# Attention without a gate: transposed scores and their exponentials one slot later

## What is computed

```
scores = einsum('bhqd,bhkd->bhqk', q, k) * scale
attn   = softmax(scores, axis=-1)
out    = einsum('bhqk,bhkd->bhqd', attn, v)      # then  out @ wo (+ bo)
```

## Time and profile before

| | |
|---|---|
| median of the runs | 5419.02 us |
| the profiled execution's own time | 5403.87 us |
| its span, first to last instruction | 5402.1 us |
| granted TensorE clock over the span | 0.866 of full speed |
| busy share PE / VectorE / ScalarE / GpSimd | 75% / 79% / 51% / 60% |
| f0, a1 and x1 together | about 1560 us |

### The profile page before, as it was taken

One profiled execution on the slowest core, in us unless ns is written; L12 is line 12 of the kernel. 1 busy time (PEld: TensorE's weight loads), 2 busy tenths in 40 slices (PEclk: granted clock), 3 DMA queues, 4 the chain that ended last, 5 costly groups with the idle time before them and its releaser, 6 DMA issues. The chain is left out here.

```text
span 5402.1 us, 104475 instructions
## 1 busy us (share of the span) xinstructions
PE 4058.6 (75%) x29692; PEld 2332.1 (43%) x29692; DVE 4293.4 (79%) x8421; ACT 2777.7 (51%) x6469; POOL 3230.1 (60%) x3458
## 2 busy tenths in 40 slices
PE   5888778887888778874888678883555787788853
PEld 2333333333333333332666446663554665566632
DVE  5999999999999999995788867764255777666668
ACT  4555555555555555552777533444563445344435
POOL 5888888888888888874777633325453222233335
PEclk8998998889989999886999878995786888899975
DMA  2111111011111111111666366654125555376521
GB/s 84 67 46 57 69 69 69 38 67 69 69 57 45 69 69 69 42 61 34 111 106 105 62 111 106 109 90 151 55 88 98 94 95 93 70 120 111 104 56 31
DMA packets 320201, 420.84 MB, mean 78 GB/s; under 512 B 40000, under 2 KB 301713, under 8 KB 309137
## 3 DMA queue, kind: packets, MB, share of 16 engines
q1 hardware_dynamic: 315536, 408.35, 32.6%
q0 software_dynamic: 4352, 8.95, 0.5%
HBM read 307.65 MB, written 109.58 MB: 77 GB/s over the span
## 5 line engine op out<-in xcount | busy, mean ns | idle before, releaser
L2202 POOL TENSOR_TENSOR m_h<-m_dtu,m_Bb 128x512 f32<-128x512 f32 x1024 | 1595.2, 1586 | 150.8 <-PE bank L1835 148.2
L1835 PE MATMUL bank<-m_h,ident 128*128 128x512 f32 x2048 | 1254.2, 704 | 400.3 <-DVE m_h L2101 393.2
L1835 PEld LDWEIGHTS bank<-m_h,ident 128*128 128x128 f32 x2048 | 373.1, 212 | 1084.6 <-DVE m_h L2101 930.6
L2095 DVE TENSOR_TENSOR_SCAN m_h<-m_dA,m_h 128x512 f32<-128x512 f32 x512 | 771.3, 1506 | 0.5
L2101 DVE TENSOR_TENSOR m_h<-m_h,bank 128x512 f32<-128x512 f32 x1024 | 672.6, 657 | 13.1 <-PE bank L1828 13.1
L2095 DVE TENSOR_TENSOR_SCAN m_h<-bank,m_h 128x512 f32<-128x512 f32 x512 | 620.6, 1212 | 16.3 <-ACT bank L1983 9.5
L1983 ACT ACTIVATE m_dA<-m_dt,m_A 128x512 f32<-128x512 f32 x512 | 366.9, 717 | 354.5 <-DVE m_h L2095 347.7
L1983 ACT ACTIVATE bank<-m_dt,m_A 128x512 f32<-128x512 f32 x512 | 352.5, 688 | 379.2 <-DVE m_h L2095 273.3
L688 DVE TENSOR_REDUCE x_nm<-bank 128x4 f32<-128x308 f32 x512 | 242.7, 474 | 177.9 <-PE bank L359 175.0
L531 ACT ACTIVATE x_sm<-bank,x_nm 128x77 f32<-128x77 f32 x1024 | 317.7, 335 | 62.3 <-DVE x_nm L688 61.9
L688 DVE TENSOR_REDUCE f_nm<-bank 128x4 f32<-128x512 f32 x256 | 175.8, 688 | 123.8 <-PE bank L359 123.1
(11 more groups left out here) (425 smaller groups left out, 10404.8 us busy)
## 6 DMA issues: line engine op xcount, KB each, us to landing
m_Bb<-m_B SPq DMA_DIRECT2D x32, 4096.0 KB, 12.1
x_Ks<-x_k_parts SPq DMA_DIRECT2D x32, 462.0 KB
x_q_parts<-x_qp SPq DMA_DIRECT2D x32, 384.0 KB, 4.1
x_Qs<-x_q_parts SPq DMA_DIRECT2D x32, 384.0 KB
f_Ks<-f_k_parts SPq DMA_DIRECT2D x16, 768.0 KB
a_Ks<-a_k_parts SPq DMA_DIRECT2D x16, 768.0 KB
x_xp<-x_stage SPq DMA_DIRECT2D x32, 256.0 KB
x_Qs<-x_q_parts SPq DMA_DIRECT2D x32, 256.0 KB
```

Of the source, the lines that this page charges most:

```text
L1835: pe.matmul(banks[4 + c], ident[:], h[:, k % RING, :], start=(s == 0), stop=(s == NS - 1)).then_inc(s_ya.sem, 1)
L2095: v.tensor_tensor_scan(h[:, k % RING, :], decays[k % AHEAD], h[:, k % RING, :], 0.0, ALU.mult, ALU.add).then_inc(s_h.sem, 1)
L2202: pool.tensor_tensor(h[:, k % RING, :], dtu[:, d, c, :], Bb[:, d, s, :], ALU.mult).then_inc(s_dB.sem, 1)
```

## The change

The transposed scores and their exponentials of chunk c run two slots behind the slot of `turn_max` instead of one. The maxima's transpose, the plain scores, the values and everything else keep their place. A helper says which item and chunk belong to a slot; for the gated stage x0 nothing is changed.

```diff
+    T_AT = 2
...
+        def turned_chunk(c):
+            return (1, c - T_AT) if c >= T_AT else (2, c - T_AT + 4)
...
@@ tensor, step
-                elif c == 0:
-                    if live(2):
-                        shifted(b - 2, (lb - 2) % 8, 3)
-                    if live(1):
+                else:
+                    k, chunk = turned_chunk(c)
+                    if live(k):
+                        shifted(b - k, (lb - k) % 8, chunk)
+                    if c == 0 and live(1):
                         turn_max(b - 1, (lb - 1) % 8)
-                elif live(1):
-                    shifted(b - 1, (lb - 1) % 8, c - 1)
@@ scalar, step
-                    if c == 0 and live(2):
-                        exp(b - 2, (lb - 2) % 8, 3)
-                    if c > 0 and live(1):
-                        exp(b - 1, (lb - 1) % 8, c - 1)
+                    k, chunk = turned_chunk(c)
+                    if live(k):
+                        exp(b - k, (lb - k) % 8, chunk)
```

## The result

| | before | after |
|---|---|---|
| median of the runs | 5420.0 us (5417.2 to 5424.55, 4 runs) | 5328.65 us (5324.35 to 5332.97, 4 runs) |
| ratio | | 0.9836 (95%: 0.982 to 0.9852) |
| the profiled execution's own time, span | 5403.87, 5402.1 us | 5331.78, 5330.1 us |
| granted TensorE clock | 0.866 | 0.875 |

The changed kernel is 91 us faster; 45 were forecast (5374 us, range 5345 to 5400). Sign and place were right; the gain is twice what was forecast. The two profiled executions differ by 72 us, because the one of before was 16 us under its median and the one of after 3 us over.

What follows compares the result with a forecast made beforehand. PE was taken as mostly the bound, sometimes waiting for VectorE. Gains 21 (a1) + 18 (x1) + 1 (f0) - 1 (drain) + 5 (clock) = 44, rounded to 45 us, gave 5374 us, range 5345 to 5400.

Steps and rivals of the forecast that it cites:

- a1: 21: Stage a1: direct gain of 21 us from PE's vanished waits for `nmT`, 10 at loop turns, 10 inside turns, 1 at the end.
- the clock: 5: Mainly a1's loop turns: less idle time brings PE back to 2.4 GHz sooner; 5 us taken, bounds 0 and 7.
- f0: 1.1 us at most: Stage f0: PE's wait for `nmT` at L377 is 1.1 us in all, of which 1 us was taken as gain.
- x1: 18: Stage x1: all 19.6 us of PE's waits for `nmT` vanish, less 1.6 for the stack load: 18 us gained.
- ceiling of the direct gain: PE's waits for `nmT` at L377 in f0, a1 and x1, in all 58.2 us, 1.1% of the time.
- Place 2, last items of a group, 0 us: Last items of a1's groups, 11 waits, about 6.6 us: PE arrives earlier and waits longer for VectorE at L367; 0 us.
- The wait at `turn_max` up to 49: In a1, PE's wait at L367 for `add_residual` was to rise from 42.8 to about 49 us.
- Exponentials hidden, stack load in time: Exponentials keep 2.3 us of slack; x1's stack load has 13.9 us for at most 12.8, so both still fit.
- Clock of a1 at 0.88: Sign expected in the profile after: a1's granted clock at 0.88, from 0.87 before.
- The clock gives more: Rival: a1's clock comes to 0.91, half-clock time falls by 46 us; gain 59 us, 5360 us. Chance 0.14.
- VectorE takes a1's gain: Rival: PE arrives earlier but waits longer at L367 for `add_residual`; a1 gives 5 or less, 5396 us. Chance 0.22.
- f0 unchanged within 2 us, wrong if by more than 3: Stage f0 as control: length unchanged within 2 us; the forecast counts as wrong if it changes by more than 3 us.

## Why the prediction was wrong in size

The mechanism held at each place where it could be looked up. To see the sizes I took, in both profiles, the distances between the starts of successive `scores` (one per slot), over the ten groups in the middle of a stage. They need no modelled end of a matmul.

*The forecast's own sum went wrong in "a1: 21" and "the clock: 5", in "f0: 1.1 us at most", and in "x1: 18", where it had no term for stalls without a releaser.* Three things were mis-sized:

1. **The idle time that a row shows for PE is less than the wait costs.** A matmul's end is modelled and covers the beginning of the wait behind it. In f0 the profile had 1.1 us for `nmT`. A slot 1 of f0 before and after:

```profile
3335.95 0.40 PE L359 MATMUL bank<-f_Ks,f_Qs 128*128 128x128 bf16 x4
...
3337.69 0.39 PE L359 MATMUL bank<-f_Ks,f_Qs 128*128 128x128 bf16 x4
```

```profile
3337.86 0.40 PE L364 MATMUL bank<-f_Ks,f_Qs 128*128 128x128 bf16 x4
...
3339.27 0.39 PE L364 MATMUL bank<-f_Ks,f_Qs 128*128 128x128 bf16 x4
```

   1.74 us before and 1.41 after, with idle time of 0.17 us shown in it before. Over the slots at full clock it is 1.74 and 1.40: 0.34 us in each of 16 groups, 5.4 us, where the rows have 1.1. In x1 slot 1 as a rule lost 0.95 us where the row has 0.76. A slot 1 of x1, before and after:

```profile
4980.59 0.32 PE L359 MATMUL bank<-x_Ks,x_Qs 128*128 128x77 bf16 x4
...
4982.86 0.30 PE L359 MATMUL bank<-x_Ks,x_Qs 128*128 128x77 bf16 x4
```

```profile
4878.33 0.31 PE L364 MATMUL bank<-x_Ks,x_Qs 128*128 128x77 bf16 x4
...
4879.66 0.30 PE L364 MATMUL bank<-x_Ks,x_Qs 128*128 128x77 bf16 x4
```

   2.27 us became 1.33. The "ceiling of the direct gain", 58.2 us from the waits' sum, was no ceiling.

2. **The clock.** Time at half clock fell by 62 us in a1 and 14 in f0, where the forecast had 17 in a1 (3.4 for each of five turns) and named 46 as a rival. A wait of 0.3 to 0.7 us behind one of 1.6 to 2.2 us at `turn_max` brought more half clock than the long one does alone: with the long waits as they were and mostly short ones gone, 27 us of it vanished in a1 (the copy of `nmT` moved ahead). In f0 slots 2 and 3 behind `turn_max` went from 2.00 and 2.92 us to 1.30 and 2.57 in every other group. At the 0.25 to 0.44 us per us measured above at single places, 62 and 14 us are 16 to 27 and 4 to 6 us of time, an estimate. The forecast's price of 1.4 for 3.4 lies in that range; its amount of half clock was far too low.

3. **The stalls of x1.** In the profile x1 gained 21.7 us: as a rule slot 1 0.95 and slot 9 0.81 a group, less 0.39 given back in slot 3, where VectorE's `norm` runs beside GpSimd. Timed alone it gained 38.8 (31 to 51). Stalls without a releaser differ from execution to execution, at 7 to 8 us a turn, and are fewer with the change: x1 with neither order nor maxima touched took 426 to 446 us in five profiles, with the change 397 to 416 in five. The means are 29 us apart, and PE's idle time without a releaser in x1 is 27 us on average in the first five and 20 in the others, so about 7 of the 29 are stalls. Why they are fewer isn't shown.

Term by term, with the clock's share as estimated: a1's 45.6 us are the turns' 10.4 (10 forecast: right), some 16 to 27 for the clock (5), and 8 to 19 for the rest, in part hidden under modelled ends (11). f0's 11.8 are 5.4, then 4 to 6, and at most 3 that nothing carries (1). x1's 21.7 stand against 18, the timed 38.8 include the stalls and the noise of that run.

The other steps, in order:
- *Place 2, last items of a group, 0 us*: right for the wait. Their slots at full clock took 3.10 and 3.27 us before and as much after; what they gained, 1.24 us a turn, was time at half clock.
- *The wait at `turn_max` up to 49*: 44.1. *A new wait of 1.5 us five times at L359*: 9.9 us in 7, 1.4 on average.
- *Exponentials hidden, stack load in time*: right at two slots. One more slot showed room for the load, and in a1 none for the exponentials (10.2 us). The last group of a1 waits 1.7 us for its stack, 0.9 was forecast.
- *VectorE's stall at the turn stays*: right, 2.76 us.
- *Clock of a1 at 0.88*: 0.92, the rival's 0.91. "The clock gives more" was the case that came nearest, though its 5360 us was still 31 us high, since it kept the other two terms.
- *VectorE takes a1's gain*: fell for this change; it is what stops a1 when `turn_max` moves too.
- *f0 unchanged within 2 us, wrong if by more than 3*: that sign failed, by 11.8 us in the profile and 7.8 timed. f0 was no control: it had the same wait, which the rows show at a fifth of its size (1.1 of 5.4 us).

## What to carry to other kernels

Size a wait of TensorE by the distance between the starts of the work before and behind it, not by its row of idle time, and don't take the sum of such rows for a ceiling when there are many short ones. Count a short wait that comes soon after a long one at its length and at the half clock that it may bring, and get the price of half clock from the same place of the same kernel at both levels. An instruction that waits for another engine belongs behind as much independent work as the next deadline allows; where the other engine is the bound, as in a1, that ends.

## What the runs showed of the hardware

- Raising the clock from 0.92 to 0.96 in two stages by matmuls that nobody reads gave no time (5334.56 against 5317.69 us). At single places an us at half clock cost 0.25 to 0.44 us, where 0.5 would be the whole difference between 1.2 and 2.4 GHz.
- Writing out a loop of PE moved stalls of 21 to 24 us and did not remove them. In straight code all 17 of 1.5 us and more stood within 4 instructions of a multiple of 256, counted as above.
- A `norm` of x1 that falls beside a certain GpSimd operation lasts as long as that one. Eleven of 59 do, before as after, but in slot 1 before, where PE waited anyway, and in slot 2 after, and slot 3 became longer. VectorE and then GpSimd in the changed kernel (both lists: start, duration):

```profile
4880.24 1.28 DVE L749 TENSOR_SCALAR x_xr<-x_r,x_stat,x_var 128x128 f32<-128x128 f32 x1 [0.50 <-POOL x_var L899]
4885.65 0.33 DVE L749 TENSOR_SCALAR x_xr<-x_r,x_stat,x_var 128x128 f32<-128x128 f32 x1
...
4880.17 1.27 POOL L892 TENSOR_TENSOR x_xr<-x_xr,x_bob 128x512 f32<-128x512 f32 x1
```

  The same operation takes 0.33 us alone and 1.28 beside the other: both end at 4881.4 to 4881.5.
